# A graph attention layer and a 32-expert layer on one core: running 36 expert blocks inside the last six attention steps

## What is computed

```python
def _L0_gnn_ref(h, adj, W, a):
    Wh = h @ W                                   # 8192 x 256
    e = (Wh @ a1)[:, None] + (Wh @ a2)[None, :]
    e = jnp.where(e > 0, e, ALPHA * e)
    e = jnp.where(adj > 0, e, MASK_VAL)
    return jax.nn.elu(jax.nn.softmax(e, axis=1) @ Wh)
def _L0_ffn_ref(x, router_w, router_b, W1, b1, W2, b2):
    idx = jnp.argmax(xf @ router_w.T + router_b, axis=-1)      # one of 32 experts
    h = jax.nn.relu(jnp.einsum('nd,ndh->nh', xf, W1[idx]) + b1[idx])     # 256 -> 64
    return jax.nn.relu(jnp.einsum('nh,nhd->nd', h, W2[idx]) + b2[idx])   # 64 -> 256
x = x + _L0_gnn_ref(_layernorm(x), adj, L0_gnn_W, L0_gnn_a)
x = x + _L0_ffn_ref(_layernorm(x), ...)
```

## Time and profile before

| | us |
|---|---|
| median of three runs | 1185.75 |
| lowest, highest | 1184.41, 1191.76 |
| span of the profiled execution (first to last instruction) | 1177.2 |
| busy in that span: PE, DVE, ACT, POOL | 884.0, 891.8, 796.2, 655.2 |
| median less span | 8.55 |

### The profile page before, as it was taken

One profiled execution on the slowest core, in us unless ns is written; L12 is line 12 of the kernel. 1 busy time (PEld: TensorE's weight loads), 2 busy tenths in 40 slices (PEclk: granted clock), 3 DMA queues, 4 the chain that ended last, 5 costly groups with the idle time before them and its releaser, 6 DMA issues.

```text
span 1177.2 us, 24953 instructions
## 1 busy us (share of the span) xinstructions
PE 884.0 (75%) x4321; PEld 558.7 (47%) x4389; DVE 891.8 (76%) x4327; ACT 796.2 (68%) x1339; POOL 655.2 (56%) x700
## 2 busy tenths in 40 slices
PE   2777728788888878888788878876878765568995
PEld 1545514454444444544444444543544444346674
DVE  5788637888888888888788888876887876555563
ACT  1544639788878888888678887866887821146663
POOL 3555445565556556655566656654655656236664
PEclk9999959999999999999899999988998986679998
DMA  7678679999999999999899999988998995035551
GB/s 258 249 277 316 250 278 370 359 379 382 366 375 377 366 372 378 380 359 379 328 354 377 381 375 374 384 314 306 383 373 316 329 249 130 25 112 162 174 167 59
DMA packets 84715, 357.33 MB, mean 304 GB/s; under 512 B 26006, under 2 KB 52591, under 8 KB 68289
## 3 DMA queue, kind: packets, MB, share of 16 engines
q1 hardware_dynamic: 56226, 296.78, 67.9%
q0 software_dynamic: 27712, 60.06, 14.9%
q10 hardware_dynamic: 736, 0.05, 0.0%
HBM read 343.67 MB, written 32.05 MB: 319 GB/s over the span
## 4 chain that ended last, share of the span: by engine, by line
DVE 27%; DMA 22%; issue 21%; PE 9%; POOL 6%; DVEq 2%; POOLq 0%; ACT 0%; ACTq 0%
DMA regions<-x,posu 13%; DMA G_all<-wh_table,idx 7%; POOL G_all L617 4%; DVE top_word L900 2%; PE psO L1718 2%; DMA out_x<-raw_all,tok 2%; DVE xn L1170 2%; PE psO L1591 2%; POOL out_x L679 1%; DVE begun L1070 1%; DVE lidx L1185 1%; DVE oh L1193 1%; DMA wh_table<-mean_sb 1%; DVE el L1144 1%; DVE lmax L1180 1%
## 5 line engine op out<-in xcount | busy, mean ns | idle before, releaser
L617 POOL DMA_INDIRECT G_all<-wh_table,idx x384 | 397.7, 1036 | 137.8 <-issue 131.0
L725 ACT ACTIVATE sg<-raw_all,minus_tiny 128x1024 fp8e4<-128x1024 int32 x256 | 311.5, 1217 | 0.1
L728 ACT ACTIVATE sg<-raw_all,minus_half 128x1024 fp8e4<-128x1024 int32 x256 | 311.4, 1216 | 0.0
L1516 PE MATMUL psO<-word_no,share 128*128 128x512 bf16 x827 | 220.5, 397 | 3.7 <-issue 0.9
L639 POOL DMA_INDIRECT regions<-x,posu x64 | 67.4, 1053 | 209.2 <-DVE idx L1062 111.8
L1591 PE MATMUL psO<-G_all,diag 128*128 128x256 f32 x640 | 162.9, 404 | 22.3 <-DVE diag L1127 22.3
L1591 PEld LDWEIGHTS psO<-G_all,diag 128*128 128x128 f32 x640 | 123.6, 201 | 64.5 <-issue 48.3
L1525 PE MATMUL psF<-sg,fold_w 128*128 128x512 bf16 x512 | 136.5, 390 | 7.5 <-DVE top_word L900 2.7
L1516 PEld LDWEIGHTS psO<-word_no,share 128*128 128x128 bf16 x885 | 90.7, 107 | 86.4 <-issue 15.4
L758 ACT ACTIVATE pr<-ee,nmx 128x16 f32<-128x16 f32 x64 | 19.7, 308 | 153.9 <-DVE nmx L1118 153.9
L900 DVE MAX8 top_word<-psF 128x8 f32<-128x256 f32 x256 | 103.0, 425 | 15.4 <-remote 9.6
(11 more groups left out here) (227 smaller groups left out, 1901.7 us busy)
## 6 DMA issues: line engine op xcount, KB each, us to landing
raw_all<-in_adj SPq DMA_DIRECT2D x128, 2048.0 KB
raw_all<-regions SPq DMA_DIRECT2D x84, 130.0 KB, 2.1
wh_table<-G_all POOLq DMA_DIRECT2D x8, 1040.0 KB, 11.8
x_sb<-in_x SPq DMA_DIRECT2D x8, 1024.0 KB, 5.8
G_all<-wh_table,idx POOLq DMA_INDIRECT x384
regions<-pad_row SPq DMA_DIRECT2D x32, 130.0 KB
x_sb<-in_L_ffn_W SPq DMA_DIRECT2D x4, 512.0 KB
x_sb<-in_L_ffn_W SPq DMA_DIRECT2D x8, 256.0 KB
```

The costliest lines, as they stand in the source:

```text
L617: pool.indirect_dma_start(out=G[par][:, k, :], out_offset=None, in_=table[:, :], in_offset=bass.IndirectOffsetOnAxis(ap=idx[par][:, k:k + ...
L725: act.activation(sign_of[par][q][0], raw_of[b][q % 2][0], ACT.Identity, bias=minus_tiny[:, 0:1], scale=TINY, saturate=False)
L728: act.activation(sign_of[par][q][1], raw_of[b][q % 2][1], ACT.Sign, bias=minus_half[:, 0:1], saturate=False).then_inc(a_sg, 1)
L1516: pe.matmul(psO[par][:, :], share[:, :], word_no[:, 0:2, :].rearrange("p q w -> p (q w)"), start=True, stop=True)
```

## The change

While 58 strips are placed (after step 59, constant SNAP), DVE now makes a first plan of up to EARLY = 36 full blocks (`early_plan`, 29 instructions). SP loads all expert weights in its step 59, waits for that plan and for the 58 scatters, and then loads the 36 blocks with one padding write behind each of the first 32. The four other engines run the same block stages as before, with lags of up to three, at two points of each step from 60 to 65: 39 block steps in eleven chunks of 5, 4, 4, 4, 4, 4, 4, 3, 3, 2 and 2. The early blocks have one PSUM tile each for transposes, hidden layer and output, and `weighted_sum` uses psO[0] alone from step 60 on. The plan after step 65 leaves out what the early one took (`base_rest`, `first_rest`), and the loop runs over the rest.

```diff
+EARLY = 36
...
+    SNAP = NS - LAG - 1
+    CHUNKS = {(NS - LAG, 1): 5, (NS - LAG + 1, 0): 4, (NS - LAG + 1, 1): 4, (NS - LAG + 2, 0): 4, (NS - LAG + 2, 1): 4,
+              (NS - LAG + 3, 0): 4, (NS - LAG + 3, 1): 4, (NS, 0): 3, (NS, 1): 3, (NS + 1, 0): 2, (NS + 1, 1): 2}
...
+        early = Blocks(first=0, plan=early_i, psX=[psF[0][:, 0:D]] * 2, psH=[psF[1][:, 0:P]] * 2, psY=[psO[1][:, 0:D]] * 2)
...
+        def early_blocks(u, part, stages):
+
+            if isinstance(u, int) and (u, part) in CHUNKS:
+                i0 = sum(n for at, n in CHUNKS.items() if at < (u, part))
+                for i in range(i0, i0 + CHUNKS[u, part]):
+                    run_blocks(i, i % RING, i // RING, early, stages)
...
             def step(u, par, do, strip):
                 if do.ahead:
                     load_strip(u + LAG + 1, strip)
-                if isinstance(u, int) and NS - LAG <= u < NS:
-                    load_weights(u - NS + LAG)
-                    load_pads(u - NS + LAG)
+                if isinstance(u, int) and u == SNAP:
+                    for part in range(LAG):
+                        load_weights(part)
+                    load_early()
...
                     gather_tail(u + 1, 1 - par)
+                early_blocks(u, 0, [(store_block, TAIL)])
                 if do.post:
                     inverse_std(u - 1, 1 - par)
+                early_blocks(u, 1, [(store_block, TAIL)])
                 if do.place:
                     scatter(u - 2, par)
...
+                if not isinstance(n, int) or n + of.first >= STORES:
+                    v.wait_ge(y_out[r % STORES], turn * (16 * RING // STORES) + r // STORES * 16)
...
                 if do.fetch:
                     indices(u + 1, 1 - par)
                     rows_of_slots(u + 1, 1 - par)
+                early_blocks(u, 0, stages)
                 if do.attend:
                     slot_scores(u, par, half_up(u, par) * GATHERS)
...
                 if do.prepare:
                     slots_of_rows(u + 2, par)
+                early_blocks(u, 1, stages)
                 if do.place:
                     place_logits(y)
...
+                if isinstance(u, int) and u == SNAP:
+                    early_plan()
...
-            make_plan(0)
+            make_plan(0, base_rest, first_rest)
...
             def step(u, par, do):
+                early_blocks(u, 0, stages)
                 if do.attend:
                     tail_scores(u, par)
...
+                early_blocks(u, 1, stages)
                 if do.place:
                     ranks(u - 2)
```

More of the change, by code:

```diff
@@ L30 @@
 NO_TOKEN = 1.0e6
+EARLY = 36
+Blocks = namedtuple("Blocks", "first plan psX psH psY")
 Does = namedtuple("Does", "ahead search decode attend fetch prepare post place")
@@ L234, in gat_moe @@
         psXn = [psT, psO[0], psO[1]]
-        psX = [psF[0], psW[0]]
-        psH = [psL, psW[1]]
+        early = Blocks(first=0, plan=early_i, psX=[psF[0][:, 0:D]] * 2, psH=[psF[1][:, 0:P]] * 2, psY=[psO[1][:, 0:D]] * 2)
+        rest = Blocks(first=EARLY, plan=plan_i, psX=[psF[0][:, 0:D], psW[0][:, 0:D]], psH=[psL[:, 0:P], psW[1][:, 0:P]],
+                      psY=[psO[0][:, 0:D], psO[1][:, 0:D]])
         const_in = sem("const_in")
@@ L364, in rounds_of_six, with sum_of @@
             peeled(NS - LAG - 2, NS + 2)
+        def sum_of(u, par):
+            return psO[0] if isinstance(u, int) and u > SNAP else psO[par]
         def half_place(strip, h):
@@ L382, in gat_moe, with run_blocks @@
         TURNS = BLOCKS // RING
+        def run_blocks(i, r, turn, of, stages):
+            for stage, lag in stages:
+                if not isinstance(i, int) or 0 <= i - lag < (EARLY if of is early else BLOCKS):
+                    stage(i - lag, (r - lag) % RING, of.first // RING + (turn if lag <= r else turn - 1), of)
+        def early_blocks(u, part, stages):
[3 more added lines that the diff above has]
+                    run_blocks(i, i % RING, i // RING, early, stages)
         def blocks_loop(eng, stages):
[L388 to L391, removed]
             eng.wait_ge(v_plan, PLAN_STEPS)
@@ L395, in blocks_loop @@
             for r in range(RING):
-                step(r, r, 0)
+                run_blocks(r, r, 0, rest, stages)
             with eng.Fori(1, TURNS) as turn:
@@ L668, in _ @@
             with pool.If(flag > 0):
+                for k in range(STORES):
+                    pool.wait_ge(y_out[k], 16 * (EARLY // STORES))
+                    pool.nop(nofuse=True)
                 def dense(t, par):
@@ L768, in count_tail, with copy_xT, copy_w1, hidden @@
                                ACT.Copy).then_inc(a_tail, 1)
+            def copy_xT(n, r, turn, of):
+                act.wait_ge(pe_xb, n + (of.first + 1))
+                act.activation(xTb[r % 2][:, :, :].rearrange("p h n -> p (h n)"), of.psX[r % 2], ACT.Copy).then_inc(a_xb, 1)
+            def copy_w1(n, r, turn, of):
+                e = act.value_load(of.plan[0:1, bass.ds(n + P, 1)], min_val=0, max_val=E - 1)
+                if not isinstance(n, int) or n + of.first >= 2:
+                    act.wait_ge(a_hT, n + (of.first - 1))
+                act.activation(w1_b[r % 2][:, 0:DH * H + 1], w1_sb[:, bass.ds(e, 1), :].rearrange("p o n -> p (o n)"),
+                               ACT.Copy).then_inc(a_w1, 1)
+            def hidden(n, r, turn, of):
+                act.wait_ge(pe_h, n + (of.first + 1))
+                act.wait_ge(a_w1, n + (of.first + 1))
+                act.activation(hT[r % 2][0:H, :], of.psH[r % 2][0:H, :], ACT.Relu,
+                               bias=w1_b[r % 2][0:H, DH * H:DH * H + 1]).then_inc(a_hT, 1)
+            stages = [(copy_xT, 1), (hidden, 2), (copy_w1, 0)]
             for u in range(2):
```

242 lines of the change are left out of this document (161 added, 81 removed).

## The result

Four runs of each kernel, taken side by side, give 1210.95 us (1201.94 to 1212.54) for the changed kernel against 1185.24 us (1184.41 to 1191.76): a ratio of **1.0169, 95% interval 1.0114 to 1.0223**. The change makes the kernel 1.7% slower. (All ratios leave out executions more than 1.5% above the fastest of the same kernel, so a ratio can differ a little from the quotient of the medians printed beside it.) The profiled execution of the changed kernel took 1211.33 us, and its span is 1209.0 us.

The account below looks back on a forecast made before the run. The prediction took DMA to bound the adj stretch and a latency chain across engines to bound the last steps. Added terms of 77.7 us less 53.6 saved gave +24.1, about 1210 us, range 1186 to 1230.

Parts of the forecast that it names:

- Saved, 53.6 us: Final block loop: 36 early blocks taken off leave four turns instead of seven, saving 53.6 us.
- Plan, +6.8: Early plan on DVE between steps 59 and 60, ahead of the scores of step 60: adds 6.8 us.
- the chunk of step 60, +6.5: Chunk of five between PE's logits and DVE's placing in step 60: adds 6.5 us.
- First chunks of steps 61 and 62, +12.3 and +13.6: Before the scores, rows wait for an output store behind six gathers on POOL: adds 12.3 and 13.6 us.
- Second chunks of 61 to 63, +7.0 each: Between logits and placing, PE and DVE in lockstep: 6.3 plus 0.7 for a store, 21.0 us in all.
- The chunk of 63, +6.5, step 64, +7.0, step 65, +6.0: First chunk of step 63 without long stall, then chunks of steps 64 and 65: add 6.5, 7.0 and 6.0 us.
- SP and padding, -2.0: Weights asked for together in step 59, padding writes leaving the adj stretch: DVE's gather wait shrinks, 2.0 us less.
- R1: Rival, chance 0.13: early matmuls fill PE's pauses, attention steps run at 2.4 GHz, saving 9 us: 1201 us.
- R2: Rival, chance 0.11: first chunks of steps 61 and 62 do not wait for the store, 14 us less: 1196 us.
- R3: Rival, chance 0.13: block steps fill PE's pauses in steps 60 to 65, costing under 1.20 us each: 1166 us.
- R4: Rival, chance 0.03: the 36 blocks are not all full, final loop needs five turns, 17.9 us back: 1228 us.

## Why the prediction was right, point by point

**Saved, 53.6 us: too large by 3.3.** 48 loads and 45 stores are left in the loop, as forecast, and the last stretch is shorter by 50.3 us. I took three whole turns from the middle of the loop. Of the missing 3.3 us, 1.9 lie behind the last store (13.6 us from its start to the end of the span, against 11.7 before). Another 2.0 are pace: from the first norm to the last store the loop is 51.6 us shorter, not 53.6; a store came every 1.48 us before and comes every 1.51 now. The stretch from the last scatter to the first norm is 0.7 us shorter, which makes up the difference.

**Plan, +6.8, and the chunk of step 60, +6.5.** The first plan runs from 975.71 us, and DVE opens the next work at 982.46: 6.75 us, as forecast; with nothing else changed it cost 7.1. Step 60 as a whole is +12.9 against 13.3.

**First chunks of steps 61 and 62, +12.3 and +13.6.** From opening to scores it is 14.2 us in step 61 (14.5 forecast) and 13.0 in step 62 (14.5). The second stall, and the scores behind it:

```profile
1032.64 0.17 DVE L1120 TENSOR_SCALAR idx<-keys 128x5 uint32<-128x5 f32 x1
...
1045.28 0.15 DVE L1321 CAST tok<-raw_all 128x1 uint32<-128x1 f32 x1 [5.83 <-DMA out_x<-raw_all,tok]
1045.35 0.41 DVE L1322 SCALAR_TENSOR_TENSOR raw_all<-psO,raw_all 128x256 f32<-128x256 f32 x1
1045.68 0.22 DVE L1156 TENSOR_SCALAR slot_s<-slot_col,G_all 128x11 f32<-128x11 f32 x1
```

I had taken the same 14.5 for both. The store landed 2.57 us after its start at 1042.71 here and 3.65 us after its start in step 61; the range of 2.5 to 3.6 in the sum held the first and just missed the second. The place of the stores on POOL was confirmed as the cause by the exchange there, and the prediction's price of a chunk without the stall, 6 us, is 5.1 and 6.4 in that run.

**Second chunks of 61 to 63, +7.0 each: too large.** From scores to logits the three steps have grown by 5.7, 6.8 and 4.7 us, 17.2 instead of 21.0. Step 61, where DVE stood still for 2.87 us ahead of the logits before:

```profile
1021.73 0.41 DVE L1313 TENSOR_SCALAR xnb<-raw_all 128x256 f32<-128x256 f32 x1
1025.37 0.15 DVE L1321 CAST tok<-raw_all 128x1 uint32<-128x1 f32 x1 [3.24 <-PE psO L1792]
...
1029.98 0.15 DVE L1321 CAST tok<-raw_all 128x1 uint32<-128x1 f32 x1 [0.47 <-PE psO L1792]
...
1030.38 0.18 DVE L1233 TENSOR_TENSOR lg<-psL,rb_sb 128x32 f32<-128x32 f32 x1
```

The fourth rows wait 0.47 us, for PE. The 0.7 us that I had added for a store in each of these chunks did not come: the first of these stores starts at 1026.65 us, one row after its data, with no gathers ahead of it. With 6.3 the sum would have been 18.9.

**The chunk of 63, +6.5, step 64, +7.0, step 65, +6.0.** From the logits of step 62 to the scores of step 63 it is 6.9 us more than before; the steps 64 and 65 grew by 7.7 and 6.1.

**SP and padding, -2.0.** Not shown. DVE's wait for the gathers in step 59 is 2.04 us here against 4.24, but the scatter of strip 57 moves by 15 us from one execution to the next, and such a row says nothing on the change.

**Two errors that cancelled.** The profiled span came to 1209.0 us, and I had said 1201.3. The median came to 1211, and I had said 1210. I had added 8.55 us for what lies around a span, and that is only 2.3 us (1211.33 - 1209.0). Executions of the kernel before lie 1.8 us above their spans (1182.18 against 1180.4), so the profiled one took about 1179 us and was quick by some 6; where it was quick is not shown. The span came 7.7 us above my figure and the addition 6.2 us below: that the median fits to 1 us is luck. The difference that was forecast, +24.1, came out as +24.5 in the traces and +25.7 in the medians; there too its two sides erred alike, 74.9 us added instead of 77.7 and 50.3 saved instead of 53.6. A median is to be held against medians; the difference between a span and a median is not what lies around the span.

**The rivals.** *R1, the clock stays up:* the granted clock of the stage did rise, from 0.64 to 0.80, but not where attention would gain by it. The weighted sums of steps 61, 62 and 63 in the changed kernel (ten matmuls):

```profile
1019.10 4.08 PE L1712 MATMUL psO<-G_all,diag 128*128 128x256 f32 x10 [0.37 <-DVE diag L1185]
...
1048.82 4.58 PE L1712 MATMUL psO<-G_all,diag 128*128 128x256 f32 x10 [0.36 <-DVE diag L1185]
...
1073.15 4.06 PE L1712 MATMUL psO<-G_all,diag 128*128 128x256 f32 x10 [0.58 <-DVE diag L1185]
```

None is near the 2.40 us of step 58. The clock of single stretches shows where it rose (columns as above): the second chunk of step 61, then in step 63 the scores and softmax ahead of the sum, and the sum itself:

```profile
1023.20:1030.40 7.20, 6.34 (x40) 4.93 (x39) 2.99 (x12) 4.24 (x13) 2.57 (x3) 1.00 0.36 106
1071.00:1073.10 2.10, 0.36 (x2) 0.30 (x2) 1.96 (x7) 0.81 (x3) 0.91 (x1) 1.00 0.62 188
1073.15:1077.20 4.05, 4.05 (x11) 3.25 (x12) 2.04 (x10) 0.00 (x0) 0.65 (x1) 0.58 0.01 4
```

This chunk runs at the full clock. In step 63 it is still full while PE, waiting for scores and softmax, works for 0.36 of 2.10 us, and over the sum it is 0.58. The rule of the Trainium skill that I quoted ("TensorE: Matmul & The Clock Gate", section "HAM oscillation — how this bites in real kernels") is borne out for steps 61 and 62, where PE stood idle for 7.77 and 6.02 us ahead of the scores; that step 63 would gain by it is not, since its sum takes 4.06 us. *R2* fell with the exchanged stores. *R3:* its break-even of 1.20 us for a block step was the right question. The answer by chunks is 1.74 in the changed kernel, 1.44 with the stores first and 1.42 for twelve late ones; in one piece, with its own waits for stores, it is 1.68. With each engine's piece placed apart it is 0.49 to 0.71, on the other side. *R4* did not come: four turns.

## What to carry to other kernels

An idle share of 40 or 50% in a stage that is one chain across engines is not room for work: a piece put at one fixed point of every engine's list lengthened the chain here by its full length. A block step cost 1.4 us in chunks and 0.5 to 0.7 us when each engine got its part where it would wait, with a buffer more for norms and two more for outputs. Before adding a DMA to an engine's list, count what is issued ahead of it there: six gathers of 1.3 us made a buffer come free some 8 us late, and DVE stood behind it. And compare stretches that begin at the same event, not whole spans, when the change sits behind a long stage that wanders by itself; but begin early enough to take in all that the change moved (the plan in step 59 was missed so).

## What the runs showed of the hardware

*Chips differ by up to 8%, and not in every stage.* The same kernel takes 1182, 1245 and 1277 us on three chips, in one session on each. The steps from the scatter of strip 57 to that of strip 63 take 60.8 us on the first and on the third (in all; single steps differ by up to 1.9); all of the difference lies ahead of them (the scatter of strip 57 comes at 969 and at 1045 us) and in the plan and the block loop (147.1 and 171.9 us from the last scatter). From 200 to 900 us the two chips show (first the first chip, then the third; columns as above):

```profile
200.00:900.00 700.00, 562.54 (x2724) 330.29 (x2776) 585.84 (x3037) 564.02 (x841) 407.30 (x417) 0.97 0.95 364
```

```profile
200.00:900.00 700.00, 535.75 (x2476) 310.69 (x2525) 539.00 (x2767) 521.26 (x765) 370.09 (x379) 0.92 0.89 333
```

333 GB/s instead of 364. What DVE waits for in the block loop, kernel before, first chip (us in total, times, longest):

```profile
DVE tok L1453 <- PE psO L1718: 36.4, 63, 2.0
DVE tok L1453 <- DMA out_x<-raw_all,tok: 10.3, 14, 1.8
DVE xnb L1445 <- DMA raw_all<-regions: 5.9, 4, 4.5
```

and on the third chip:

```profile
DVE xnb L1445 <- DMA raw_all<-regions: 35.9, 40, 4.5
DVE tok L1453 <- PE psO L1718: 33.8, 43, 2.2
```

There the block loads are late, 40 times instead of 4, at a lower rate of data (121 GB/s against 143). The chain of waits runs there over SP's own steps between two loads. The longest pieces of it, kernel before, third chip:

```profile
1123.96 0.72 SPq L512
...
1125.45 0.70 SPq L516
...
1126.20 0.71 SPq L512
```

Not all are so long: SP's issue of a load takes 0.33 us in the median on both chips, but up to 0.72 us on the third and at most 0.37 on the first. Why, and whether that is the cause of the late loads, was not tried.

*Kept fillers do hold the clock.* With fillers in every step the weighted sums of steps 61 to 63 run in 2.32 us, and the granted clock over each of them is 1.00, the high of the two levels; without them they take 3.92 to 4.61 us at 0.50 to 0.61, and with expert blocks in their place 4.06 to 4.58 at 0.52 to 0.58. Blocks that come in groups did not do what the spread fillers did, with a stall ahead of the sum (steps 61 and 62) or without one (step 63).
